# Moving projections, routing, loads and reciprocals in a three-layer attention and expert kernel

## What is computed

```python
x = x + attn(ln(x))                        # A: q, k rotated; softmax over 512 keys
n = ln(x)
y = softmax(causal(q k'))  v               # B
y = y + softmax(qc kc')  vc                # C: kc, vc from ctx_512, qc from n
x = x + y @ Wp + bp
z = ln(x)
gate = softmax(z @ Wg); idx = argmax(gate)
loc = place of the token in its expert's queue; valid = loc < 256
x = x + where(valid, relu(z @ w1[idx]) @ w2[idx] * gate[idx], 0)
```

## Time and profile before

| | us |
|---|---|
| median of 3 runs (1564.07 to 1566.87) | 1565.12 |
| the profiled execution | 1563.6 |
| its span, first to last instruction | 1561.8 |

### The profile page before, as it was taken

The page is one execution under the profiler, slowest core; times in us unless marked ns, Lnnn a source line. Parts: engine busy times, 40 slices in busy tenths (PEclk is TensorE's granted clock), DMA queues, the critical chain, the costliest instruction groups (busy, mean ns, idle before and its releaser), DMA issues.

```text
span 1561.8 us, 37676 instructions
## 1 busy us (share of the span) xinstructions
PE 1415.5 (91%) x14538; PEld 634.1 (41%) x14538; DVE 1194.4 (76%) x2434; ACT 1055.4 (68%) x2139; POOL 653.2 (42%) x535
## 2 busy tenths in 40 slices
PE   3799999999999999999999999999899988599997
PEld 1223322332333434434334343343343432279896
DVE  6788888888877777877977878779678785547774
ACT  2387788788778677677676776776767757236562
POOL 2555574466423421336245333362353221235553
PEclk9699999999999999999999999999999999799999
DMA  6435534433323434334333332343334301167771
GB/s 180 128 117 137 147 97 124 133 115 106 94 62 104 111 88 108 91 91 107 87 93 86 105 103 64 91 109 84 84 92 109 84 21 44 42 233 259 271 243 59
DMA packets 119478, 175.80 MB, mean 113 GB/s; under 512 B 26273, under 2 KB 85895, under 8 KB 114696
## 3 DMA queue, kind: packets, MB, share of 16 engines
q1 hardware_dynamic: 111376, 158.50, 35.7%
q0 software_dynamic: 5888, 14.24, 2.8%
q10 hardware_dynamic: 2048, 0.83, 0.2%
HBM read 102.33 MB, written 51.18 MB: 98 GB/s over the span
## 4 chain that ended last, share of the span: by engine, by line
PE 58%; DVE 18%; ACT 8%; DMA 6%; issue 5%; POOL 2%; SPq 1%; DVEq 0%; POOLq 0%; ACTq 0%
PE psO L742 13%; DVE negmax L1221 11%; PE psM L467 11%; PE psS L765 10%; PE psK L467 7%; PE psK L796 6%; ACT probs L1030 6%; PE psS L467 4%; DMA stack<-mrows 3%; DMA recipB<-recip_scratch 2%; PE psK L694 2%; PE psM L832 1%; DVE xn L1169 1%; DVE mrows L1323 1%; PE psM L881 1%
## 5 line engine op out<-in xcount | busy, mean ns | idle before, releaser
L1221 DVE TENSOR_REDUCE negmax<-psS 128x1 f32<-128x512 f32 (+3 forms) x1536 | 868.8, 615 | 222.8 <-PE psS L765 113.4
L1030 ACT ACTIVATE probs<-psK 128x512 f32<-128x512 f32 (+3 forms) x1536 | 755.4, 546 | 309.6 <-PE psK L796 183.9
L742 PE MATMUL psO<-probs,V 128*32 128x256 f32 (+1 forms) x5632 | 440.3, 384 | 10.3 <-ACT U L1022 8.8
L765 PE MATMUL psS<-stack 48*128 48x512 f16 (+3 forms) x1536 | 282.6, 364 | 45.4 <-DVE negmax L1221 41.5
L796 PE MATMUL psK<-stack 50*128 50x512 f16 (+3 forms) x1536 | 276.1, 356 | 17.4 <-DMA stack<-mrows 11.4
L765 PEld LDWEIGHTS psS<-stack 48*128 48x128 f16 x1536 | 74.1, 93 | 357.0 <-DVE negmax L1221 294.9
L742 PEld LDWEIGHTS psO<-probs,V 128*32 128x32 f32 x5632 | 112.3, 108 | 192.2 <-issue 127.8
L1439 POOL TENSOR_TENSOR rstd<-lnt,minus_half 128x4 f32<-128x4 f32 x24 | 24.8, 1033 | 247.1 <-DVE lnt L1161 247.1
L796 PEld LDWEIGHTS psK<-stack 50*128 50x128 f16 x1536 | 75.9, 94 | 49.4 <-issue 17.9
L1571 POOL DMA_INDIRECT out_dram<-stack,put_to x32 | 76.8, 2399 | 17.8 <-issue 9.1
L467 PE MATMUL psM<-xT,wx 128*128 128x512 f16 x288 | 76.7, 382 | 1.6 <-DVE mrows L1323 0.6
(11 more groups left out here) (192 smaller groups left out, 2017.9 us busy)
## 6 DMA issues: line engine op xcount, KB each, us to landing
spare<-in_L_ffn_w_dram SPq DMA_DIRECT2D x32, 1024.0 KB, 6.4
parts_scratch<-parts SPq DMA_DIRECT2D x192, 128.0 KB
stack<-parts_scratch SPq DMA_DIRECT2D x96, 256.0 KB
stack<-parts_scratch SPq DMA_DIRECT2D x96, 128.0 KB
packed<-U SPq DMA_DIRECT2D x192, 64.0 KB
recipB<-recip_scratch SPq DMA_DIRECT2D x48, 256.0 KB
shared<-shared SPq DMA_DIRECT2D x48, 128.0 KB, 2.1
probs<-back_scratch POOLq DMA_DIRECT2D x16, 258.0 KB, 3.2
```

Source lines behind the costliest of these rows:

```text
L742: mm = nc.tensor.matmul(psO[32 * i:32 * i + 32, q0:q1], v_of(par)[:, kt, 2 * g + i % 2 + PAIRS * (i // 2), :], probs[:, (unit + i % 2) % P ...
L765: mm = nc.tensor.matmul(psS[:, banks[hh], 0:n], stack_of(par, 0)[rows, hp, qt * P:(qt + 1) * P], stack_of(par, 1)[rows, hp, 0:n], start=Tr ...
L1030: nc.scalar.activation(probs[:, t % P_RING, i, q0:T], psK[:, S_BANKS[t][i], q0:T], ACT.Exp, scale=SM_SCALE / (1 if b.kind == "A" else WSCA ...
L1221: nc.vector.tensor_reduce(negmax[:, g % 2, at:at + 1], psS[:, S_BANKS[u // 2][j], 0:n], AX_X, ALU.max, negate=True).then_inc(s["max_done"], 1)
```

## The change

In B units two of the eight loads go from slot 8 to 14. In C units the projections end at slot 14 instead of 17, the router's steps run three to four slots earlier, the loads of slots 9 and 10 go to 14 and the earlier ones close up, the stores begin at 14, the normalisation goes from 11 to 16, and all eight scatters are issued within the unit, from slot 27 on. In the tail the sums are moved ahead of the products; the reciprocals are no longer written to DRAM and read back, but multiplied on DVE by a constant that puts each on its place in 512 columns (`recip_wide`), and spread over the features by two fp32 matmuls with a 0/1 matrix (`head_rows`), which DVE builds in slot 4; the normalisation reads the result from PSUM. The four low weight splits of the first two experts move: one behind the layer norm, three behind the scatter indices. The GpSimd's copy of the residual waits for the layer norm, and the four row scatters go ahead of the gate's product.

```diff
--- before.py
+++ after.py
@@ the table of slots, SLOTS_OF
     "BB": {"v0": (0,), "v1": (2,), "xT0": (8,), "xT1": (10,), "proj0": (14, 15), "proj1": (16, 18),
...
-           "ln": (0, 0, 4, 5), "ln_mid": 1, "load": (1, 1, 1, 5, 6, 6, 8, 8), "split": (10, 11, 14, 19, 20, 23),
+           "ln": (0, 0, 4, 5), "ln_mid": 1, "load": (1, 1, 1, 5, 6, 6, 14, 14), "split": (10, 11, 14, 19, 20, 23),
...
-           "load": (1, 2, 3, 6, 7, 8, 9, 10), "split": (8, 10, 13, 15, 18), "store": (12, 14, 17, 20), "recip": 8, "norm": 11,
+           "load": (1, 1, 2, 3, 6, 6, 14, 14), "split": (8, 10, 12, 13, 15), "store": (14, 15, 17, 19), "recip": 8, "norm": 16,
...
@@ -369,6 +369,10 @@
         zT = shared[:, 2048:3072].rearrange("p (f t) -> p f t", f=FT)
         staging = shared[:, 2048:3072].rearrange("p (s t) -> p s t", s=2)
         back = shared[:, 3072:3072 + TT * (D + 2)].rearrange("p (t d) -> p t d", t=TT)
+        wide = wx[:, :, :, :, :].rearrange("p j a k n -> p (j a k n)").bitcast(F32)
+        head_rows = wide[:, 0:FT * P].rearrange("p (f n) -> p f n", f=FT)
+        head_of, chunk_of = wide[:, 256:272], wide[:, 272:280]
+        recip_wide = wide[:, 512:1024].rearrange("p (c t) -> p c t", c=8)
         bias_vT = sb("bias_vT", [P, 3, FT], F32)
         bias_o = sb("bias_o", [P, 2, D], F32)
         bias_qk = sb("bias_qk", [P, 6, FT], F32)
...
@@ -614,13 +619,20 @@
...
+                        if not b.kind:
+                            for ft in range(FT):
+                                sp.dma_start(sums[PART * ft + HD * g:PART * ft + HD * (g + 1), :],
+                                             U[PART * ft:PART * (ft + 1):3 * HD, g % 2, :]).then_inc(last_sums, 16)
+                            for ft in range(FT):
+                                sp.dma_start(packed[2 * HD * g:2 * HD * (g + 1), ft, :],
+                                             U[PART * ft + HD:PART * ft + 3 * HD, g % 2, :]).then_inc(s["packed_1"], 16)
+                        for ft in range(FT if b.kind else 0):
                             sp.dma_start(packed[2 * HD * g:2 * HD * (g + 1), ft, :],
                                          U[PART * ft + HD:PART * ft + 3 * HD, g % 2, :]).then_inc(s[f"packed_{g % 2}"], 16)
                             sp.dma_start(sums[PART * ft + HD * g:PART * ft + HD * (g + 1), :],
                                          U[PART * ft:PART * (ft + 1):3 * HD, g % 2, :]).then_inc(s[f"packed_{g % 2}"], 16)
 
-                    if t == b.recip_slot and b.prev:
+                    if t == b.recip_slot and b.prev and b.kind:
                         sp.wait_ge(s["recip_done"], b.at("recip_done", 1))
                         sp.dma_start(recip_dram.rearrange("h (c t) -> (h c) t", c=8), recip[:, :]).then_inc(s["recip_stored"], 16)
                         sp.wait_ge(s["recip_stored"], b.at("recip_stored", 16))
@@ -697,8 +709,15 @@
 
                 if (name, j) == ("out", 0):
                     pe.wait_ge(s["max_done"], total["max_done"])
-                    for done, k, n in (("recip_done", 1, 6), ("recip_stored", 16, 12), ("recip_in", 16 * FT, 5), ("attn_mul", 1, 4),
-                                       ("attn_sum", 1, 2)):
+                    pe.wait_ge(s["recip_done"], b.at("recip_done", 1))
+                    keep_warm(psS[:, 0, :], 4)
+                    pe.wait_ge(rows_set, 4)
+                    pe.wait_ge(wide_set, 1)
+                    for ft in range(FT):
+                        nc.tensor.matmul(psS[:, 1 + ft, :], head_rows[:, ft, :], recip_wide.rearrange("p c t -> p (c t)"),
+                                         start=True, stop=True).then_inc(recip_spread, 1)
+                    keep_warm(psS[:, 0, :], 4)
+                    for done, k, n in (("attn_mul", 1, 4), ("attn_sum", 1, 2)):
                         pe.wait_ge(s[done], b.at(done, k))
                         keep_warm(psS[:, 0, :], n)
                 if (name, j) == ("zT", 0):
@@ -1220,19 +1239,30 @@
                         dve.wait_ge(s["scores_q"], b.at("scores_q", k + 1))
                         nc.vector.tensor_reduce(negmax[:, g % 2, at:at + 1], psS[:, S_BANKS[u // 2][j], 0:n], AX_X, ALU.max,
                                                 negate=True).then_inc(s["max_done"], 1)
+                    if b.n == 24 and t == 4:
+                        nc.vector.tensor_reduce(head_of, ident.rearrange("p (h c) -> p h c", c=8), AX_X, ALU.add).then_inc(rows_set, 1)
+                        nc.vector.tensor_reduce(chunk_of, ident.rearrange("p (h c) -> p c h", c=8), AX_X, ALU.add).then_inc(rows_set, 1)
+                        dve.wait_ge(rows_set, 2)
+                        for ft in range(FT):
+                            nc.vector.tensor_copy(head_rows[:, ft, :].rearrange("p (h d) -> p h d", d=HD),
+                                                  head_of[:, 8 * ft:8 * ft + 8, None].to_broadcast([P, 8, HD])).then_inc(rows_set, 1)
                     if t == b.recip_slot and b.prev:
 
                         dve.wait_ge(s["packed_0"], b.at("packed_0"))
-                        dve.wait_ge(s["packed_1"], b.at("packed_1", PACKED))
+                        dve.wait_ge(s["packed_1"], b.at("packed_1", PACKED if b.kind else 0))
+                        if not b.kind:
+                            dve.wait_ge(last_sums, 16 * FT)
                         need(dve, s["recip_stored"], b.at("recip_stored"))
                         nc.vector.reciprocal(recip[:, :], sums[:, :]).then_inc(s["recip_done"], 1)
                     if b.n == 24 and t == 5:
 
-                        for which in range(2):
-                            expert_lo(0, 0, which)
-                        dve.wait_ge(s["recip_in"], b.at("recip_in", 16 * FT))
+                        dve.wait_ge(s["recip_done"], b.at("recip_done", 1))
+                        nc.vector.tensor_tensor(recip_wide, recip[:, None, :].to_broadcast([P, 8, 64]),
+                                                chunk_of[:, :, None].to_broadcast([P, 8, 64]), ALU.mult).then_inc(wide_set, 1)
+                        dve.wait_ge(s["packed_1"], b.at("packed_1", PACKED // 2))
                         for ft in range(FT):
-                            o = nc.vector.tensor_tensor(recipB[:, ft, :], packed[:, ft, :], recipB[:, ft, :], ALU.mult)
+                            dve.wait_ge(recip_spread, ft + 1)
+                            o = nc.vector.tensor_tensor(recipB[:, ft, :], packed[:, ft, :], psS[:, 1 + ft, :], ALU.mult)
                         o.then_inc(s["attn_mul"], 1)
                         dve.wait_ge(s["attn_mul"], b.at("attn_mul", 1))
                         for ft in range(FT):
@@ -1242,8 +1272,8 @@
                             dve.wait_ge(s["attn_hi"], b.at("attn_hi", ft + 1))
                             nc.vector.tensor_tensor(attn[:, 1, ft, :], recipB[:, ft, :], attn[:, 0, ft, :], ALU.subtract
                                                     ).then_inc(s["attn_out"], 1)
-                        for which in range(2):
-                            expert_lo(1, 1, which)
+                    if b.n == 24 and t == 16:
+                        expert_lo(0, 0, 0)
                     if ln and (t in b.ln_steps or t == b.ln_mid) and b.n == -2:
                         if t == b.ln_steps[0]:
                             dve.wait_ge(x0_in, 16)
...
@@ -1377,6 +1408,9 @@
                             chain(nc.vector.tensor_scalar(rs[:, 7, :], rs[:, 5, :], 1000.0 * CAP, None, ALU.add), 16)
                         if t == b.chain_slots[5] and not b.kind:
                             places()
+                            expert_lo(0, 0, 1)
+                            for which in range(2):
+                                expert_lo(1, 1, which)
 
 
@@ -1534,16 +1568,21 @@
                     if b.route and t == b.slots["back"]:
                         need(pool, s["back_scattered"], b.at("back_scattered"))
                         need(pool, s["x_out"], b.at("x_out", 0 if b.kind else 2))
+                        if not b.kind:
+                            pool.wait_ge(s["ln_out"], b.at("ln_out", 1))
                         gb = b.routed()
                         nc.gpsimd.tensor_copy(back[:, :, 0:D], X[:, bass.ds(gb, 1), :].rearrange("p o (t d) -> p (o t) d", t=TT)
                                               ).then_inc(s["back_set"], 1)
                     if b.route and t == b.scatter_slots[0]:
                         pool.wait_ge(s["index_out"], b.at("index_out", 1))
+                        pool.wait_ge(rows_zero, 16 * 33)
+                        if not b.kind:
+                            for part in range(TT):
+                                scatter(part)
                         nc.gpsimd.tensor_tensor(back[:, :, D], rs[:, 3, :], gate_scale[:, :], ALU.mult).then_inc(s["gate_set"], 1)
-                        pool.wait_ge(rows_zero, 16 * 33)
                         pool.wait_ge(s["gate_set"], b.at("gate_set", 1))
                     if b.route:
```

(4 more changed lines are left out.)

17 lines of the change are left out of this document (8 added, 9 removed).

## The result

The changed kernel takes 1541.9 us (median of 4 runs, 1538.5 to 1544.9), the kernel before 1565.5 in the same series: ratio 0.985, 95% interval 0.983 to 0.988. 23.6 us are gained, 16.6 were forecast (1548.5). The profiled execution of the changed kernel takes 1542.1 (span 1540.3), 21.5 less than that of before. I call units 8 to 22 the middle, and the work from the end of the last attention product (1326.3 before, 1312.1 after) the tail.

A forecast was written before the change was run, and what follows sets the result against it. No single engine bounds it: attention units run at the pace of loops through PE, DVE and ACT. Gains 10.5 + 1.5 - 2.1 + 0.5 + 2.5 + 3.7 = 16.6 gave 1547.0 profiled, 1548.5 by median; range 1539 to 1557.

The forecast's parts named there:

- the rival with the clock up and a quick tail: No clock fall in C units, spreading matmuls at full clock, slots neutral: 1541.1 us, chance 0.15.
- Loads behind the rows: B and C units: rows of maxima issued ahead of loads and stores, ending PE's waits for them; 10.5 us gained.
- GpSimd in C units: Normalisation moved behind the projections' splits, ending ACT's waits on those splits; 1.5 us gained.
- Projections and routing earlier: C units: same instructions four slots earlier, crowding some slots; 0.3 us lost in each of seven units, 2.1.
- rivals of crowded slots and of a slow routing chain: C units lose 1.5 each, 1557 us, chance 0.12; DVE and PE wait on each other in routing, 1571.6, chance 0.05.
- Scatters: C units: scatters start three slots earlier, and DVE work no longer delays the rows of slot 29; 0.5 us gained.
- The clock: TensorE's clock falls at the logits of units 11, 17 and 19, costing 4.9 us; half taken as gained, 2.5.
- Tail, first part: After the last attention unit: earlier sums, and matmuls replacing the reciprocals' store, load-back and broadcast; 4.2 us gained.
- Tail, second part: Two weight splits leave the place before the residual sum, 2.6 us gained; GpSimd's copy waits for the layer norm, 0.3.
- Tail, third part: Three splits beside the row scatters hold each scatter until a split ends, delaying the expert layers; 2.8 us lost.
- The rival built on it: Row scatters go free of the splits, so the expert layers start 2.8 us earlier: 1545.1 us, chance 0.08.
- Clock at the first expert: PE idles longer before the first expert's 36 matmuls, which may lose more by the clock; 0.6 us lost.

The follow-up runs named there:

- e1: Kernel before with only the last two loads of B and C units and the first two C stores moved behind the rows: 1552.7 us, ratio 0.989.
- e9: Changed kernel with B and C loads and the first C store back in their old slots ahead of the rows: 1546.4 us, ratio 0.989.
- e3: Changed kernel with C units' projections, splits, logits, count, routing chain and scatters back in their old slots: 1553.2 us, ratio 0.991.
- e10: Changed kernel with the C units' normalisation on GpSimd back at slot 11 from 16: 1545.1 us, ratio 0.988.
- e6: Changed kernel with the last stage's four weight splits moved out of the row scatters' time: 1539.0 us, ratio 0.984.
- e2: Changed kernel with the B and C slot tables of the kernel before, so only the tail is new: 1561.1 us, ratio 0.996.
- e5: The changed kernel run again unaltered, beside three further runs: 1544.8 us, ratio 0.987.
- e8: Changed kernel with weight splits out of the scatters' time, 16 fillers before the reciprocals, and no slot-25 fillers in C units: 1538.0 us, ratio 0.983.
- e7: Changed kernel with 16 more filler matmuls between the last attention product and the wait for the reciprocals: 1542.2 us, ratio 0.985.
- e4: Changed kernel without the two filler matmuls in slot 25 of C units: 1540.9 us, ratio 0.983.

## Why the prediction was right, and where its terms were off

Direction, main mechanism and range held; the gain was 23.6 instead of 16.6. The time lies beside the 1541.1 of the rival with the clock up and a quick tail, but not by its mechanism: the clock still fell in three C units and over the spreading matmuls, and only its third condition, slots that cost nothing, came true. Term by term:

- *Loads behind the rows, 10.5.* Right in cause and size: 10.4 by slot 15 (in C units 6.3 more before than the 1.92 that the slot has in e1, in B units 4.8 more before than after, less 0.7 in unit 8, where the slot got longer), 9.4 by e9.
- *GpSimd in C units, 1.5.* The size is near (2.1 in slots 19 and 20 of units 13, 15 and 19), the cause wrong. In the old order the loads' move alone ends that wait (e1), and the normalisation at 16 would have cost 1.2 a unit (e3). In the new order it must be there (e10).
- *Projections and routing earlier, -2.1.* This is the step that failed: I set the crowded slots 12, 19 and 20 against emptied ones and let the crowding win by 0.3 a unit. The filled slots cost 1.2 and the emptied ones bring 1.6 at full clock (unit 17, e6 against e1, the normalisation's and the scatters' move included), 0.2 a unit over six units and minus 0.7 in unit 9: plus 0.5 to 0.7 in all. The rivals of crowded slots and of a slow routing chain fall with it.
- *Scatters, +0.5.* About 0.6 between the two profiles (slots 5 to 7 of the B units), and 2.6 to 3.1 against e1, e2 and e3, while the new place loses nothing in eight profiles. Their landing sets when the next unit's layer norm may write `xn`. As e2 has the tables of before, the term is worth 0.6 to 3.1 by execution, and that it came out near 0.5 is luck. I had priced their packets beside the rows of slot 29 and not looked at who waits for them to land.
- *The clock, +2.5.* 5.0 before and 3.0 after in the profiled units, 2.0. The size is luck. That the falls would go with the waits for rows is refuted: e1 has three of them with 2.4 us of such waits left, e9 has 9.5 us of waits and no fall, and e5 has the falls in other units than the same kernel's first profile. Their number changes too, from none in the C units of e6 to five in e8. What decides it stays open. The kernel before ran from 1559 to 1578 while the changed kernel kept to 1538 to 1546; how much of that spread is the clock's, and how much that of the waits for rows and scatters, was not separated.
- *Tail, first part, 4.2.* 4.2. The fp32 matmuls, bounded by the earlier trace rows alone, came out at 1.8 each at half clock against my 1.9, and 0.95 at full clock (e7), as taken.
- *Tail, second part, 2.6 + 0.3.* 2.7 and 0.9. The second is 0.6 larger, because the copy on GpSimd no longer runs beside the layer norm, whose `xn` takes 1.38 instead of 2.03.
- *Tail, third part, -2.8.* 2.7 lost, by the mechanism of the earlier trace rows. It is worth 3.1 when undone (e6). The page "SBUF — State Buffer" of the Trainium skill, in "Who interferes with whom", infers that descriptor generation goes free of a `tensor_tensor`, which takes the read side only; these scatters beside a `scalar_tensor_tensor` with two SBUF inputs don't (2.39, 1.80 and 1.91 against 0.97), and the measurement decides. The rival built on it falls.
- *Clock at the first expert, -0.6.* Wrong in sign, plus 1.7: e1 has the short duration behind the old tail and four kernels with the new tail have the long one, so neither the change nor the longer idle time ahead of it sets it. Nor were unit 23 (0.9) and the load of the rows (0.5) in my sum.

Of the 7 us missed (7.2 by the profiles, units 0 to 7 left out), some 2.7 lie in the order of the C units, 2.3 at the first expert, 0.9 in unit 23, 1.3 in the small terms of the tail and 0.6 in the GpSimd term; the clock of the middle took 0.5 back.

## What to carry to other kernels

A small transfer that an engine will wait for is to be issued ahead of the bulk ones on its queue, and a large vector operation kept out of the time in which GpSimd writes scatters that others wait for; both are found by reading what stood in front of the late one, not by shares of busy time. When a step is moved, price the slots that it leaves as carefully as those that it fills, and ask who waits for it to land: here the emptied slots gave more than the full ones took, and the earlier scatters paid because the next unit's layer norm waits for them. A fixed position is right only for one order of the rest (the normalisation at slot 11 or 16), so edits that lean on each other are tried together.

## What the runs showed of the hardware

- An fp32 matmul of 128x512 takes 0.95 us at the upper level of TensorE's clock and 1.8 at the lower one (two in 1.90 and 3.62).
- An indirect scatter of 128 rows (0.97 us of GpSimd) is held by a `scalar_tensor_tensor` on VectorE of 128x2048 with two SBUF inputs: 1.8 to 2.4 us. A copy on GpSimd is held too: the residual's (L1574, 128x1024), 1.03 us before, takes 2.93 in the changed kernel, where the first split runs beside it, and ends 0.9 behind it, as the scatters do. Nothing waits for that copy.
- Sixteen fillers, 3.6 us, in a stretch that PE had idled through kept the clock up (e7, e8), and what followed ended 2.6 us sooner (e7).
- The granted clock of the same stretch of the same kernel differs from one execution to the next: a fall at the logits costs 0.9 to 1.0 us against the same unit at full clock (after, e4, e5), and the first expert's 36 matmuls take 4.09 or 5.7 to 5.8 us.
